# Values three slots behind the scores, each tile's tail one slot later, and layer norm's chain in two slots: one decoder layer on one core

## What is computed

```
h = rms_norm(proj(rms_norm(emb_table[x], norm_weight)))
h = h + attention(layernorm(h), wq, wk, wv, wo)    # causal, 32 query heads, 8 key/value heads, head width 16
h = h + ffn(layernorm(h), w_gate, w_up, w_down)    # down(silu(gate(x)) * up(x)), hidden width 2048
```

## Time and profile before

| | |
|---|---|
| median of 3 runs | 844.55 us (843.16 to 845.46) |
| profiled execution, whole | 845.19 us |
| its span, first to last instruction | 843.4 us |
| PE busy | 690.9 us (82%) |
| DVE busy | 450.8 us (53%) |
| ACT busy | 349.7 us (41%) |
| POOL busy | 342.1 us (41%) |
| share of PE in the chain that ended last | 57%, DVE 17%, issue 14% |

### The profile page before, as it was taken

How to read it: one execution, slowest core, us unless ns; L and a number is a source line. 1 busy time by engine, 2 the same in 40 slices (tenths; PEclk the granted TensorE clock), 3 DMA queues, 4 the chain that set the end, 5 groups by cost and what they waited for, 6 DMA issues and landing times.

```text
span 843.4 us, 15750 instructions
## 1 busy us (share of the span) xinstructions
PE 690.9 (82%) x6180; PEld 510.4 (61%) x6180; DVE 450.8 (53%) x1026; ACT 349.7 (41%) x685; POOL 342.1 (41%) x364
## 2 busy tenths in 40 slices
PE   7420244376788999899989999999999899999998
PEld 4320132154665698479847974797488648865883
DVE  6789356874663466345635563565355536543330
ACT  4400256434652275237514651565057406640330
POOL 6000454312544355436553654374347424640220
PEclk9755555577999999999999999999999999999999
DMA  8457201100001100110011002000200110000000
GB/s 330 207 197 313 78 2 29 50 1 1 2 1 41 65 2 2 52 53 2 2 56 48 2 2 91 14 2 15 79 14 1 41 52 14 2 1 26 2 1 25
DMA packets 10456, 40.33 MB, mean 48 GB/s; under 512 B 1808, under 2 KB 2576, under 8 KB 8592
## 3 DMA queue, kind: packets, MB, share of 16 engines
q1 hardware_dynamic: 5472, 20.98, 6.5%
q0 software_dynamic: 3328, 13.11, 4.9%
q10 hardware_dynamic: 1584, 5.24, 1.6%
HBM read 29.89 MB, written 9.44 MB: 47 GB/s over the span
## 4 chain that ended last, share of the span: by engine, by line
PE 57%; DVE 17%; issue 14%; ACT 5%; POOL 4%; DMA 1%; SPq 0%; ACTq 0%; DVEq 0%; POOLq 0%
PE banks L909 9%; PE banks L911 9%; PE banks L910 9%; PE banks L924 6%; PE banks L926 6%; PE banks L925 6%; DVE weights L686 5%; PE banks L844 2%; PE banks L884 2%; PE banks L885 2%; PE banks L886 2%; POOL weights_split L303 2%; DVE gate_work L674 2%; DVE ffn_weights L630 1%; PE banks L833 1%
## 5 line engine op out<-in xcount | busy, mean ns | idle before, releaser
L910 PE MATMUL banks<-xnT_and_h,ffn_weights 128*128 128x256 f16 x1024 | 283.5, 277 | 0.0
L909 PE MATMUL banks<-xnT_and_h,ffn_weights 128*128 128x256 f16 x1024 | 283.4, 277 | 0.0
L911 PE MATMUL banks<-xnT_and_h,ffn_weights 128*128 128x256 f16 x1024 | 283.3, 277 | 0.0
L303 POOL TENSOR_TENSOR weights_split<-weights,weights_split 128x512 f16<-128x512 f32 x128 | 149.9, 1171 | 111.3 <-ACT weights_split L424 99.4
L299 POOL TENSOR_TENSOR gated_split<-gate_work,gated_split 128x256 f16<-128x256 f32 x128 | 88.7, 693 | 214.1 <-ACT gated_split L418 214.0
L414 ACT ACTIVATE weights<-banks,scales 128x512 f32<-128x512 f32 x128 | 87.1, 680 | 84.5 <-PE banks L844 84.5
L911 PEld LDWEIGHTS banks<-xnT_and_h,ffn_weights 128*128 128x128 f16 x1024 | 101.5, 99 | 13.4
L910 PEld LDWEIGHTS banks<-xnT_and_h,ffn_weights 128*128 128x128 f16 x1024 | 101.4, 99 | 12.9
L909 PEld LDWEIGHTS banks<-xnT_and_h,ffn_weights 128*128 128x128 f16 x1024 | 101.3, 99 | 12.9
L424 ACT ACTIVATE weights_split<-weights 128x512 f16<-128x512 f32 x128 | 80.6, 630 | 61.1 <-DVE weights L686 61.1
L686 DVE SCALAR_TENSOR_TENSOR weights<-weights,counts_T 128x512 f32<-128x512 f32 x128 | 97.7, 764 | 10.0 <-ACT weights L414 9.9
(11 more groups left out here) (195 smaller groups left out, 958.7 us busy)
## 6 DMA issues: line engine op xcount, KB each, us to landing
ffn_weights<-in_ffn_w SPq DMA_DIRECT2D x12, 1024.0 KB, 13.8
out_rows_dram<-ffn_weights SPq DMA_DIRECT2D x16, 256.0 KB, 2.0
local_table<-gated_split ACTq DMA_DIRECT2D x4, 512.0 KB, 2.6
local_table<-xnT_and_h ACTq DMA_DIRECT2D x4, 512.0 KB, 8.8
xnT_and_h<-in_wqkv SPq DMA_DIRECT2D x1, 1536.0 KB, 8.8
gated_split<-in_projT SPq DMA_DIRECT2D x4, 256.0 KB, 4.5
ffn_weights<-in_wo SPq DMA_DIRECT2D x1, 1024.0 KB, 10.9
token_table<-weights_split ACTq DMA_DIRECT2D x1, 768.0 KB, 3.3
```

What stands on the lines that cost most here:

```text
L303: g.tensor_tensor(WTl[V % RING], E[V % RING][:, :], WTh[V % RING], ALU.subtract).then_inc(wt_lo, 1)
L909: t.matmul(o, wh, xTh[m % 2][:, c, :], start=c == 0, stop=False)
L910: t.matmul(o, wh, xTl[m % 2][:, c, :], start=False, stop=False)
L911: last = t.matmul(o, wl, xTh[m % 2][:, c, :], start=False, stop=c == DC - 1)
```

## The change

Every slot below is one of the 24 of a phase. Values of unit V are computed in slot V+3, no longer V+2, on TensorE; ScalarE's copy of a pair follows in the even slots from 4 on. The tables of the tail:

| | before | now |
|---|---|---|
| Y_SLOT | 9, 17 | 10, 18 |
| YT_SLOT | 11, 19 | 12, 20 |
| WO_SLOT | 12, 20 | 13, 21 |
| LN_SLOT (residual, statistics) | 13, 21 | 14, 21 |
| XHAT_SLOT (reciprocal root, xn) | 13, 21 (part of LN_SLOT) | 15, 21 |
| XN_SLOT | 15, 22 | 16, 23 |
| FETCH_SLOT | 14, 22 | 15, 22 |

No instruction is added or removed. From the new `if` on, all line numbers are one higher than in the kernel before.

```diff
-Y_SLOT, YT_SLOT, WO_SLOT, XN_SLOT = (9, 17), (11, 19), (12, 20), (15, 22)
-LN_SLOT = (13, 21)
-FETCH_SLOT, M_SLOT = (14, 22), (19, 3)
+Y_SLOT, YT_SLOT, WO_SLOT, XN_SLOT = (10, 18), (12, 20), (13, 21), (16, 23)
+LN_SLOT, XHAT_SLOT = (14, 21), (15, 21)
+FETCH_SLOT, M_SLOT = (15, 22), (19, 3)
...
-                    if att and s >= 3 and s % 2 == 1 and s < UPB + 3:
-                        i = (s - 3) // 2
+                    if att and 4 <= s < UPB + 4 and s % 2 == 0:
+                        i = (s - 4) // 2
...
                             link(v.tensor_scalar(st[:, 34:35], st[:, 33:34], 0.5, 0.5 * EPS_LN, ALU.mult, ALU.add))
+                        if att and s == XHAT_SLOT[k]:
                             rsqrt(st[:, 34:35], st[:, 35:36], st[:, 36:37])
...
-                    if att and 2 <= s < UPB + 2:
-                        values(n * UPB + s - 2)
+                    if att and 3 <= s < UPB + 3:
+                        values(n * UPB + s - 3)
```

## The result

| | before | after |
|---|---|---|
| median | 845.0 us (13 runs, 843.16 to 846.25) | 848.91 us (13 runs, 846.0 to 850.7) |
| ratio, 95% interval | | 1.0043 (1.0031 to 1.0055) |
| profiled execution: span | 843.4 us | 846.8 us |

What follows compares the result with a forecast made beforehand. TensorE was taken to bound blocks 2 to 7, ScalarE and VectorE blocks 0 and 1. Blocks 2 to 6 -2.5, block 7 +0.8, block 1 +1.0, block 0 +1.6: +0.9 us, 845.5 from the median; range 837 to 849.

Steps and rivals of the forecast that it cites:

- B: Slot 16, kernel before: value matmuls wait 1.26 us for ScalarE's copy of the values, costing about 1.42; claimed to go.
- C: Slot 17, kernel before: value matmuls wait 1.17 us for GpSimd's low half behind DMA issues, costing about 1.33; claimed to go.
- the sign given: Sign expected in the changed profile: no wait of value matmuls for ScalarE or GpSimd in blocks 1 to 7.
- W: Slot 16: new TensorE wait for xn, forecast 2.35 to 2.6 us, taken as 2.5; 1.33 if nothing is held.
- L647 held, L707 not: VectorE beside GpSimd's L303: two-input L647 takes 1.29 us, not 0.30; one-input, one-element L707 0.15. L647's behaviour was assumed.
- Rival 1: Slot 15: one-element operations not held by GpSimd; W 1.33, block 0 lower by 1.2, total 836.0 us; chance 0.23.
- Rival 2: xn (L711) also held, by the fetch's first DMA issue; W 2.9, total 848.3 us; chance 0.25.
- The row at 361.15: Profile row before the change: L711 takes its usual 0.55 us within a DMA issue; cited against Rival 2.
- forecast -2.5: Blocks 2 to 6: 5 x (W - 3.0), where 3.0 us a block is the loss expected to go.
- the ScalarE copies in the same parity: Tail one slot later together with ScalarE's copies: output projection's 0.65 us wait stays, move costed at nothing.
- 7 W - 16.6: Sum over all blocks: +0.9 us against the profiled execution, with W at 2.5.
- main case: Whole kernel: within 0.3% of before, for W from 2.0 to 2.73; 843.0 to 848.0 us, chance 0.52.

Runs made afterwards that it cites:

- e1_one_input: Changed kernel with L471 and L472 of the reciprocal root written with one SBUF tensor and pointer scalars instead of two SBUF tensors: 843.27 us.
- e2_xn17: Second experiment: changed kernel with XN_SLOT of the first tile 17 in place of 16: 839.21 us.
- e9_after_copy_early: Changed kernel with ScalarE's copy of the values moved ahead of the gate's high half, chain still in two slots: 845.72 us.
- e4_fetch15: Kernel before the change with only FETCH_SLOT of the first tile 15 in place of 14: 837.34 us.
- e3_chain14: Third experiment: changed kernel with layer norm's chain of the first tile whole in slot 14 (XHAT_SLOT 14 in place of 15): 837.85 us.

## Why the prediction was right, and where it fell short

**The bound and the places of the waits**: right for blocks 2 to 7. B and C left the list, and the blocks' differences have the signs forecast. Two exceptions: in block 1 the value matmuls go on waiting for ScalarE, against the sign given (none in blocks 1 to 7), and in every block slot 5 has a new small one.

**W, the wait for xn**: right in mechanism and size, 2.43 for 2.35 to 2.6. Of the two neighbours (L647 held, L707 not) the one with the same inputs was the right one, and e1_one_input shows it. Rival 1, that one element is not held, is out; its time of 836.0 was not tested, but its term of 1.2 for block 0 did not show in e1_one_input. Rival 2, that xn is held by the DMA issue, was a small truth: 0.11 us (0.55 to 0.66), not 0.4. The row at 361.15 that spoke against it was a poor guide: there the issue had begun only 0.09 us before L711. Where it had begun 0.54 us before, xn takes 0.66 in every block (e2_xn17 and e9_after_copy_early too), and where 0.42 before, 0.78 (e1_one_input, second tile).

**"So B and C go in each block"**: C by its own merit (e4_fetch15); B not. The prediction gave the copy 2.6 us more of time, but did not follow ScalarE's queue: the copy of slot 16 waits there for VectorE's gate product, which stands behind the chain. As long as W is longer this changes nothing in the time; it only falsified my expectations of the second and third experiment.

**Blocks 2 to 6**, forecast -2.5, measured -0.43: the mis-sized term. Of the 2.1 us, 1.5 are the fall of the clock in block 5 (1.49), and the rest is the copy in slot 5, 0.2 in each of five blocks, less 0.07 x 5 for W at 2.43. Per block: -3.0 + 2.43 + 0.2 = -0.37, and -0.38 was measured. The fall of the clock had no term at all: the prediction did not ask what TensorE's clock does behind a wait of this length. The step that failed reads "the ScalarE copies in the same parity": the copies keep their place beside the tail, but not beside place_max, which did not move.

**Blocks 0, 1 and 7**: +1.94, +1.26 and +0.85, forecast +1.6, +1.0 and +0.8. The bound search starts at 171.45, forecast 171.4:

```profile
171.45 2.27 DVE L572 TENSOR_REDUCE part_max<-ffn_weights 128x2 f32<-128x2048 f32 x1
```

In block 1 the parts fit as well: slots 0 to 13 are 1.95 longer (forecast +1.5), the rest 0.70 shorter (forecast 0.5). In block 0 the sum came out and the terms did not, which is partly luck. For slot 10 the prediction had +1.0, but the two halves of the split take 1.50 and 1.54 in place of 0.92 and 1.64, 0.5 more. For the second tile it had +1.8 to +2.5 from the wait for L698; the projection does start 2.1 later, counted from the block's start, but its own wait grows only from 1.55 to 1.98, while the wait for y ahead of its transposes grows from 4.93 to 7.29. The chain in one slot makes block 0 0.5 us and block 1 1.2 us shorter (e3_chain14: 77.06 and 116.25), so about 1.4 of block 0 belongs to the rest of the change.

**The number.** 7 W - 16.6 with W at 2.43 would give +0.4; the 0.2 a block in seven blocks make 1.4, the fall of the clock 1.5, the sum 3.3, and the two profiled spans differ by 3.4. So the main case was given as "within 0.3%", and its missing terms carried it to 0.43%. The prediction's bounds did not fit each other either: W from 2.0 to 2.73 gives 842.0 to 847.1 by its own sum, not 843.0 to 848.0. The time of 848.9 lies above both and near the 848.3 of rival 2, whose mechanism is not there; it falls inside the wide range because that range had been drawn to reach into rival 2, and not because the sum had the slot 5 copy and the clock.

## What to carry to other kernels

Work on VectorE with two SBUF inputs that starts while a GpSimd subtraction of this kernel is running is charged the whole remaining time of that instruction, even for one element; what starts first keeps its time. A chain of small operations meets it several times. Keep such a chain together in a slot where GpSimd is idle, rather than spreading it to let other work through. Before moving work between engines' slots to mend a wait, look at what stands ahead of the late instruction in its own queue: here one table entry (fetch) and one reordering within a slot (copy) gain 2.0% together where the whole rearrangement loses 0.4%; the copy together with the later values and tail, and the chain kept in one slot, gains 2.6%. Waits in series on one engine are not additive: removing the first hands its time to the second when that has a ready time of its own.

## What was not expected of the hardware

A halt of TensorE of 2.15 to 3.97 us can bring a stretch of 3.4 us (once 6.8) at a granted clock of 0.50, at 1.2 GHz in place of 2.4, in some executions and blocks and not in others; at 2.27 us (2.15 in block 7) in 1 or 2 blocks of 6, at 3.53 us (3.97 in block 7) in 5 of 6. A wait then costs 1.5 to 1.7 us more than its length (once 2.7). The times of the changed kernel also spread more, 4.7 us over 13 runs against 3.1 over 13 of the one before; a changing number of falls would do that, but only three executions of kernels with this wait were profiled.

The same arithmetic on one element took 0.22 and 0.16 us as a two-tensor operation and 0.27 and 0.21 with pointer scalars (one number a partition, given by its address), alone in both cases.
